# Graph layer with decayed neighbours: VectorE's differences taken straight behind the floors in every slot

## The chip, the cores and the metric

One core of one Trainium2 chip runs the kernel. The metric is the device time in microseconds (us) of one execution. An execution is measured from outside the profile; the span of the profile is the time from the first to the last recorded work of the core, and is a little shorter.

## The reference

The inputs are `x` (4096x64), a 0/1 matrix `adj` (4096x4096, about 16 ones in a row), a 64x64 weight and a bias, all float32. Cut to what matters:

```python
h = relu(layernorm(x))
support = h @ weight
mask = (adj != 0)
rank = cumsum(mask, axis=1)
deg = rank[:, -1:]
k = minimum(deg, 100)
pos = rank - (deg - k)
w = mask * where(pos > 0, 0.5 ** (k - pos), 0)
out = x + w @ support + bias
```

So each neighbour of a row is weighted by one half to the power of how many neighbours stand behind it. The running count, turned into powers of two, and the product with `support` are the work.

## The kernel before

**Tiling.** The rows of `adj` are taken in 32 groups of 128 (1 MB each). They are packed into 18 units (`SIZES`): units 0, 1, 2 and 17 hold one group, the others two. A unit's 4096 columns are walked backwards in steps of 128 columns, split into 2 or 4 chains side by side (`CHAINS`), so that a unit takes 16 (or 8) steps (`STEPS`).

**What the engines do for a unit.** GpSimd issues the load of a group (L242), eight in flight, each new one when `mask` has freed a buffer. VectorE makes 0/1 bytes of it (`mask`, L358), folds them with additions of halves (`halve_1`, `halve_2`, `halve_3`, all by L364), and scans the sums (`scan`, L399) to know how many neighbours stand behind each run of columns. TensorE starts a chain in PSUM from that (`base`, L612), and in each step adds the neighbours of one more block of columns (`count`, L624 and L626). ScalarE turns the PSUM values after each step into the bits of a power of two (`weigh`, L313, tile `powers`). TensorE multiplies these with `support` and adds up in a PSUM tile (`product`, L633, tile `acc`). `support` stands in three parts, whose three sums VectorE adds to `x` with `add_low`, `add_middle`, `add_high` (L436, L441, L446); then the rows are stored.

**Marked and plain groups.** `MARKS` says how many groups of a unit have their count marked by TensorE itself (two matmuls a step). The other groups, here called plain, are in units 5, 8, 11, 14, 15, 16 and 17. For them ScalarE writes powers of the running count alone, and VectorE makes weights of them in batches of four steps: `floor` (L415) raises values below a floor, in place, and `differ` (L425) subtracts each step's powers from the ones before. `differ` waits for `powers_ready` and for `floored`, which `floor` has signalled. A batch of four is one floor and one difference; there are 26 batches. TensorE's `product` waits for `weights_ready` ahead of each batch.

**The order of the work.** Every engine walks the same numbered slots `g`, in an order written out by hand. `STARTS[u]` is the slot in which TensorE does the base of unit u; the counts follow in the slots behind it, and the products of unit u begin `LAGS[u]` slots after its start. TensorE takes the chains of PSUM (`c = u % 3`) in order in each slot, and the first thing in a slot with products is what `before_products` waits for: for a unit's first product that is also `rows_done`, the `add_high` of unit u-4, whose `acc` tile it writes again. On VectorE batch j of unit u has its floor and its difference in slot `STARTS[u] + 4j + 5`; masks, halvings and scans of unit u stand 8 to 3 slots ahead of its start (shifted by `LEADS`), and the three additions in the slots `STARTS[u] + LAGS[u] + STEPS[u]`, one more and two more.

In this order the kernel before runs, in each slot on VectorE: the floors (L524 to L526), additions of the bias in two slots, then the masks, halvings, scans and additions of all units (L531 to L553), and last the differences:

```python
                for u in range(NU):
                    if MARKS[u] < SIZES[u] and g - STARTS[u] in range(BATCH[u] + 1, STEPS[u] + 2, BATCH[u]):
                        differ(u, (g - STARTS[u] - 1) // BATCH[u] - 1)
```

Of the kernel before, what the change touches and what calls it, by code (L numbers as in the profile page):

```python
# [5 lines left out]
def gnn_decay_kernel(nc, x, adj, weight, bias, out):  # L6
# [39 lines left out]
    SIZES = [1, 1, 1, 2, 2, 2, 2, 2, 2, 2, 2, 2, 2, 2, 2, 2, 2, 1]  # L46

    CHAINS = [4, 2, 2, 2, 2, 2, 2, 2, 2, 2, 2, 2, 2, 2, 2, 2, 2, 4]
    STEPS = [T // h for h in CHAINS]

    MARKS = [1, 1, 1, 2, 2, 0, 2, 2, 0, 2, 2, 0, 2, 2, 0, 0, 0, 0]

    STARTS = [0, 5, 6, 14, 23, 27, 34, 40, 45, 51, 57, 63, 68, 74, 80, 85, 91, 97]
    LAGS = [8, 5, 9, 10, 9, 10, 9, 8, 9, 8, 10, 12, 11, 11, 11, 10, 9, 8]

    BATCH = [4, 4, 4, 4, 4, 4, 4, 4, 4, 4, 4, 4, 4, 4, 4, 4, 4, 4]
# [4 lines left out]
    NU = len(SIZES)  # L61
# [7 lines left out]
    def taken_until(u):  # L69

        return sum(TAKEN[v] for v in range(u % FLIGHT, u, FLIGHT))

    def by_vector(u, b):
        return u in OWN_BEATS and OWN_BEATS[u][0] <= b < OWN_BEATS[u][1]
# [5 lines left out]
    def to_floor(u):  # L80

        if MARKS[u] == SIZES[u]:
            return []
        return [j for j in range(STEPS[u] // BATCH[u])
                if not all(by_vector(u, b) for b in range(first_of(u, j), BATCH[u] * (j + 1) + 1))]

    def floors_until(u):
        return sum(len(to_floor(v)) for v in range(u % FLIGHT, u, FLIGHT))
# [14 lines left out]
    with ctx:  # L103
# [110 lines left out]
        def plain(u):  # L214

            return slice(MARKS[u] * CHAINS[u] * P, SIZES[u] * CHAINS[u] * P)
# [133 lines left out]
        def _(dve):  # L350

            def mask(n):

                dve.wait_ge(adj_loaded[n % LOADS], 16 * (n // LOADS + 1))
                if n >= RING:
                    u = UNIT_OF[n - RING]
                    dve.wait_ge(chain_ready[u % FLIGHT], taken_until(u) + TAKEN[u])
                nc.vector.tensor_scalar(planes_of(n), in_planes(adj_b[:, n % LOADS, :], n), 0.0, 1.0,  # L358
                                        ALU.not_equal, ALU.mult).then_inc(mask_ready, 1)
# [11 lines left out]
            def halve_1(u):  # L371
                n, k = FIRST[u], SIZES[u]
                at = (n + SHIFT) % RING
                dve.wait_ge(mask_ready, n + k)
                halve(u, masks[:, at:at + k, :].bitcast(u16), words(part1, u, STEPS[u] // 4), halved)

            def halve_2(u):

                if CHAINS[u] == 4:
                    return  # L380
                dve.wait_ge(halved, halved_until(u) + 1)
                halve(u, words(part1, u, 4), words(part2, u, 2), halved)

            def halve_3(u):
                dve.wait_ge(halved, halved_until(u + 1))
                if u == 0:
                    dve.wait_ge(rests_ready, 2)
                if u >= SUMS:
                    dve.wait_ge(later_ready, FIRST[u - SUMS + 1])
                halve(u, words(part2 if CHAINS[u] == 2 else part1, u, 2),  # L390
                      runs_of(sums, sums_4, u)[:, :, 0:CHAINS[u] * P], sums_ready)

            def scan(u, k):

                dve.wait_ge(sums_ready, u + 1)
                if k == 0 and u >= SUMS:
                    dve.wait_ge(chain_ready[(u - SUMS) % FLIGHT], taken_until(u - SUMS) + 1)
                two = runs_of(sums, sums_4, u)[:, k, :].bitcast(u8).rearrange("q (r e) -> q e r", e=2)
                nc.vector.tensor_tensor_scan(runs_of(later, later_4, u)[:, k, ::-1], two[:, 0, ::-1], two[:, 1, ::-1],  # L399
                                             (OWN + STEP) / STEP if k < MARKS[u] else 0.0,  # L400
                                             ALU.add, ALU.add).then_inc(later_ready, 1)

            def weigh(u, b):

                c = u % FLIGHT
                dve.wait_ge(chain_ready[c], taken_until(u) + b + 1)
                nc.vector.tensor_scalar(powers[:, c, b, plain(u)].bitcast(i16), chain[c][:, plain(u)],
                                        (MAX_NEIGH + 1) * STEP, STEP, ALU.add, ALU.max).then_inc(powers_ready[c], 1)

            def floor(u, j):  # L410
                c = u % FLIGHT
                last = BATCH[u] * (j + 1)
                dve.wait_ge(powers_ready[c], taken_until(u) + last + 1)
                bits = powers[:, c, first_of(u, j):last + 1, plain(u)].bitcast(i16)
                nc.vector.tensor_scalar(bits, bits, STEP, None, ALU.max).then_inc(floored[c], 1)  # L415

            def differ(u, j):
                c = u % FLIGHT
                dve.wait_ge(powers_ready[c], taken_until(u) + BATCH[u] * (j + 1) + 1)
                done = floors_until(u) + sum(i <= j for i in to_floor(u))  # L420
                if done:
                    dve.wait_ge(floored[c], done)
                before = powers[:, c, BATCH[u] * j:BATCH[u] * (j + 1), plain(u)]
                after = powers[:, c, BATCH[u] * j + 1:BATCH[u] * (j + 1) + 1, plain(u)]
                nc.vector.tensor_tensor(before, before, after, ALU.subtract).then_inc(weights_ready[c], 1)  # L425
# [7 lines left out]
            def add_low(u):  # L433
                dve.wait_ge(acc_ready[u % ACCS], u // ACCS + 1)
                dve.wait_ge(xb_ready, 1 + (FIRST[u] + SIZES[u] > T // 4))
                nc.vector.tensor_tensor(sum_a[:, u % ACCS, 0:SIZES[u], :], parts_of(u)[:, :, 2, :], rows_of(u),  # L436
                                        ALU.add).then_inc(low_added[u % ACCS], 1)

            def add_middle(u):
                dve.wait_ge(low_added[u % ACCS], u // ACCS + 1)  # L440
                nc.vector.tensor_tensor(sum_b[:, u % ACCS, 0:SIZES[u], :], parts_of(u)[:, :, 1, :], sum_a[:, u % ACCS, 0:SIZES[u], :],  # L441
                                        ALU.add).then_inc(middle_added[u % ACCS], 1)
# [41 lines left out]
            def add_bias(f):  # L484

                dve.wait_ge(bias_ready, 1)
                rows = slice(0, T // 4) if f == 0 else slice(T // 4, T)
                n = rows.stop - rows.start
                nc.vector.tensor_tensor(x_sb[:, rows, :], x_sb[:, rows, :],
                                        bias_b.unsqueeze(1).to_broadcast([P, n, D]),  # L490
                                        ALU.add).then_inc(xb_ready, 1)
# [28 lines left out]
            for g in range(SLOTS + 4):  # L520
                for u in OWN_BEATS:
                    if by_vector(u, g - STARTS[u]):
                        weigh(u, g - STARTS[u])
                for u in range(NU):  # L524
                    if (g - STARTS[u] - 1) % BATCH[u] == 0 and (g - STARTS[u] - 1) // BATCH[u] - 1 in to_floor(u):
                        floor(u, (g - STARTS[u] - 1) // BATCH[u] - 1)  # L526
                if g == 15:
                    add_bias(0)
                if g == 46:
                    add_bias(1)  # L530
                for u in range(NU):  # L531
                    to = STARTS[u] - LEADS[u] - g
                    if u >= 3 and to == 8 and FIRST[u] > 3:
                        mask(FIRST[u])
                    if u >= 3 and to == 7 and SIZES[u] > 1:
                        mask(FIRST[u] + 1)
                    if u >= 3 and to == 6:
                        halve_1(u)
                    if u >= 3 and to == 5:
                        halve_2(u)  # L540
                    if u >= 3 and to == 4:
                        halve_3(u)
                    if u >= 3 and to == 3:
                        scan(u, 0)
                    if u >= 3 and to == 3 and SIZES[u] > 1:
                        scan(u, 1)
                    done = STARTS[u] + LAGS[u] + STEPS[u]
                    if g == done:
                        add_low(u)
                    if g == done + 1:  # L550
                        add_middle(u)
                    if g == done + 2:
                        add_high(u)  # L553
                for u in range(NU):
                    if MARKS[u] < SIZES[u] and g - STARTS[u] in range(BATCH[u] + 1, STEPS[u] + 2, BATCH[u]):
                        differ(u, (g - STARTS[u] - 1) // BATCH[u] - 1)

        @block.tensor
        def _(pe):
# [172 lines left out]
```

## Time and profile before

| what | value |
|---|---|
| median of 3 runs | 216.38 us (216.19 to 216.53) |
| the profiled execution, its own time | 216.8 us |
| span of the profile | 214.2 us |
| VectorE busy | 196.8 us, 239 instructions |
| TensorE matmuls busy | 196.7 us, 2784 instructions |
| ScalarE busy | 160.6 us, 303 instructions |
| loads of `adj` | 33.56 MB, 75.1% of the 16 DMA engines' span |

The granted clock of TensorE was full over the whole span. Busy time is the union of the recorded instructions; an engine that is busy all the time need not be the one that sets the end. What matters for a change of order is which engine waits for which, and how early each thing is ready before its user comes to it.

### The profile page before, as it was taken

The numbers are of one execution on the slowest core, as the hardware profiler recorded it, in microseconds if no ns is written. First come the engines' busy times: TensorE is split into PE (matmuls) and PEld (weight loads), VectorE is DVE, ScalarE is ACT, GpSimd is POOL, SyncE is SP. The second block draws the span as 40 slices with busy tenths as digits, with TensorE's granted clock in tenths as the row PEclk, the third lists the DMA queues.
The fourth block names the chain that finished last, engine by engine and source line by source line (L and its number), as shares of the span: only waits on it lengthen the run. The fifth ranks groups of instructions, "written<-read, shape, count | busy, mean of one in ns | idle before, by whom it ended". The sixth has DMA issues, their size and how long they took to land.

```text
span 214.2 us, 6505 instructions
## 1 busy us (share of the span) xinstructions
PE 196.7 (92%) x2784; PEld 188.0 (88%) x2784; DVE 196.8 (92%) x239; ACT 160.6 (75%) x303; POOL 29.1 (14%) x53
## 2 busy tenths in 40 slices
PE   0369979999999999999999999999999999999993
PEld 0269657997898999999999999999999999999993
DVE  1999979797979999999999999989999999998893
ACT  2442996786786988778778778789978989998720
POOL 7800000000010404010004110500000000000000
PEclk9999999999999999999999999999999999999999
DMA  6999999999999999999999999999998000000001
GB/s 203 204 217 220 216 211 216 216 219 212 218 213 221 210 218 216 213 220 216 211 222 212 217 218 215 216 217 218 221 209 174 8 12 3 12 15 3 17 0 43
DMA packets 7677, 36.09 MB, mean 168 GB/s; under 512 B 1506, under 2 KB 3298, under 8 KB 3554
## 3 DMA queue, kind: packets, MB, share of 16 engines
q0 software_dynamic: 4608, 33.56, 75.1%
q1 hardware_dynamic: 2882, 2.10, 3.8%
q8 instruction: 22, 0.36, 0.6%
q10 hardware_dynamic: 160, 0.03, 0.1%
q14 instruction: 5, 0.04, 0.1%
HBM read 68.19 MB, written 1.05 MB: 323 GB/s over the span
## 4 chain that ended last, share of the span: by engine, by line
PE 81%; DVE 7%; ACT 6%; DMA 2%; issue 1%; SPq 0%; DVEq 0%
PE acc L633 40%; PE chain L626 25%; PE chain L624 14%; ACT powers L313 3%; ACT support L296 3%; DMA x_sb<-in_x 2%; DVE masks L358 2%; PE chain L612 2%; DVE sq_sum L460 1%; DVE powers L455 1%; DVE later L399 1%; DVE row_sum L451 1%; DVE part L364 1%; DVE acc L481 0%; DVE sums L364 0%
## 5 line engine op out<-in xcount | busy, mean ns | idle before, releaser
L313 ACT ACTIVATE powers<-chain 128x512 int16<-128x512 f32 (+1 forms) x279 | 148.7, 573 | 33.6 <-PE chain L626 31.4
L633 PE MATMUL acc<-support,powers 128*128 128x192 bf16 x1024 | 159.5, 246 | 1.3 <-ACT powers L313 1.2
L626 PE MATMUL chain<-diag_own,masks 128*128 128x128 bf16 x608 | 107.1, 219 | 0.1
L624 PE MATMUL chain<-diag_past,masks 128*128 128x128 bf16 x568 | 102.2, 219 | 2.1 <-ACT powers L313 1.5
L633 PEld LDWEIGHTS acc<-support,powers 128*128 128x128 bf16 x1024 | 95.9, 98 | 4.3 <-ACT powers L313 2.4
L358 DVE TENSOR_SCALAR masks<-adj_b 128x4096 uint8<-128x4096 bf16 x32 | 72.6, 2281 | 5.0 <-DMA adj_b<-in_adj 5.0
L624 PEld LDWEIGHTS chain<-diag_past,masks 128*128 128x128 fp8e3 x568 | 55.5, 99 | 5.3 <-ACT powers L313 3.9
L626 PE MATMUL chain<-diag_step,masks 128*128 128x128 bf16 x416 | 60.1, 219 | 0.0
L626 PEld LDWEIGHTS chain<-diag_own,masks 128*128 128x128 fp8e3 x608 | 59.7, 99 | 0.3 <-issue 0.3
L626 PEld LDWEIGHTS chain<-diag_step,masks 128*128 128x128 fp8e3 x416 | 39.5, 99 | 0.0
L242 POOL DMA_DIRECT2D adj_b<-in_adj x32 | 24.5, 767 | 108.9 <-DVE masks L358 107.7
L425 DVE TENSOR_TENSOR powers<-powers 128x2048 bf16<-128x2048 bf16 x26 | 31.6, 1218 | 0.5
L399 DVE TENSOR_TENSOR_SCAN later<-sums 128x257 bf16<-128x257 uint8 (+1 forms) x32 | 21.6, 712 | 0.3
L415 DVE TENSOR_SCALAR powers<-powers 128x2048 int16<-128x2048 int16 (+1 forms) x26 | 18.7, 719 | 2.1 <-ACT powers L313 2.0
L364 DVE TENSOR_TENSOR part<-masks 128x2048 uint16<-128x2048 uint16 (+1 forms) x18 | 19.8, 1099 | 0.2
L577 PE MATMUL spare<-ident_f,powers 128*128 128x128 f32 x8 | 2.2, 425 | 9.6 <-DVE powers L455 8.8
L364 DVE TENSOR_TENSOR part<-part 128x1024 uint16<-128x1024 uint16 (+1 forms) x16 | 10.4, 651 | 0.2
L577 PEld LDWEIGHTS spare<-ident_f,powers 128*128 128x128 f32 x8 | 1.4, 216 | 9.9 <-issue 9.9
L296 ACT ACTIVATE support<-acc 128x512 bf16<-128x512 f32 x12 | 6.9, 647 | 1.2 <-DVE acc L481 1.2
L364 DVE TENSOR_TENSOR sums<-part 128x512 uint16<-128x512 uint16 (+1 forms) x18 | 7.3, 406 | 0.2
L451 DVE TENSOR_REDUCE row_sum<-x_sb 128x16 f32<-128x1024 f32 x2 | 2.4, 1220 | 5.1 <-DMA x_sb<-in_x 5.1
L612 PE MATMUL chain<-diag_base,later 128*128 128x128 bf16 x68 | 6.8, 220 | 0.0
(52 smaller groups left out, 66.3 us busy)
## 6 DMA issues: line engine op xcount, KB each, us to landing
adj_b<-in_adj POOLq DMA_DIRECT2D x32, 1024.0 KB, 35.0
x_sb<-in_x SPq DMA_DIRECT2D x2, 512.0 KB, 4.5
out<-x_sb SPq DMA_DIRECT2D x14, 64.0 KB, 5.4
out<-x_sb SPq DMA_DIRECT2D x4, 32.0 KB, 9.5
w<-in_L_gnn_weight ACTq DMA_DIRECT2D x2, 16.0 KB, 9.1
bias<-in_L_gnn_bias SPq DMA_DIRECT2D x1, 0.2 KB
```

The costliest lines, as they stand in the source:

```text
L242: pool.dma_start(adj_b[:, n % LOADS, :], adj_t[n]).then_inc(adj_loaded[n % LOADS], 16)
L296: nc.scalar.activation(steps_of(support[:, :, s, :], i), split[i][:, :].rearrange("p (t d) -> p t d", d=D), ACT.Copy).then_inc(part_ready[ ...
L313: nc.scalar.activation(powers[:, c, b, cols].bitcast(i16), chain[c][:, cols], ACT.Relu, bias=(MAX_NEIGH + 1) * STEP).then_inc(powers_ready ...
L358: nc.vector.tensor_scalar(planes_of(n), in_planes(adj_b[:, n % LOADS, :], n), 0.0, 1.0, ALU.not_equal, ALU.mult).then_inc(mask_ready, 1)
L364: return nc.vector.tensor_tensor(outs, ins[:, :, 0:h], ins[:, :, h:2 * h], ALU.add).then_inc(done, 1)
L399: nc.vector.tensor_tensor_scan(runs_of(later, later_4, u)[:, k, ::-1], two[:, 0, ::-1], two[:, 1, ::-1], (OWN + STEP) / STEP if k < MARKS[ ...
L415: nc.vector.tensor_scalar(bits, bits, STEP, None, ALU.max).then_inc(floored[c], 1)
L425: nc.vector.tensor_tensor(before, before, after, ALU.subtract).then_inc(weights_ready[c], 1)
L612: last = nc.tensor.matmul(chain[c][:, at:at + P], behind[:, hs - 1 - h], diag_base[:, :], start=(k + h == 0), stop=False, skip_group_check ...
L624: nc.tensor.matmul(chain[c][:, at:at + P], column(n, t + 1), diag_past[:, :], start=False, stop=False, skip_group_check=True)
L626: return nc.tensor.matmul(chain[c][:, at:at + P], column(n, t), diag_own[:, :] if marked else diag_step[:, :], start=False, stop=True, ski ...
L633: return nc.tensor.matmul(acc[u % ACCS][:, k * 3 * D:(k + 1) * 3 * D], powers[:, u % FLIGHT, s + 1 if k < MARKS[u] else s, at:at + P], sup ...
```

## The change

The loop over the differences moves, within each slot, from behind the masks, halvings, scans and additions to the place in front of them, behind the floors and the additions of the bias. No instruction is added or removed, and nothing moves to another slot or another engine.

```diff
                 if g == 46:
                     add_bias(1)
                 for u in range(NU):
+                    if MARKS[u] < SIZES[u] and g - STARTS[u] in range(BATCH[u] + 1, STEPS[u] + 2, BATCH[u]):
+                        differ(u, (g - STARTS[u] - 1) // BATCH[u] - 1)
+                for u in range(NU):
                     to = STARTS[u] - LEADS[u] - g
                     if u >= 3 and to == 8 and FIRST[u] > 3:
                         mask(FIRST[u])
...
                     if g == done + 2:
                         add_high(u)
-                for u in range(NU):
-                    if MARKS[u] < SIZES[u] and g - STARTS[u] in range(BATCH[u] + 1, STEPS[u] + 2, BATCH[u]):
-                        differ(u, (g - STARTS[u] - 1) // BATCH[u] - 1)
```

## Rows read from the trace of the kernel before

**Rows 1.** The page: busy by engine, and slices (tenths) of two engines and clock.
```profile
PE 196.7 (92%) x2784; PEld 188.0 (88%) x2784; DVE 196.8 (92%) x239; ACT 160.6 (75%) x303; POOL 29.1 (14%) x53
...
PE   0369979999999999999999999999999999999993
...
DVE  1999979797979999999999999989999999998893
...
PEclk9999999999999999999999999999999999999999
```

**Rows 2.** Busy time of each engine in three stretches of the span, by windows.
```profile
66.00:139.40 73.40, 72.71 (x1095) 71.60 (x1093) 73.23 (x85) 58.99 (x105) 14.27 (x13) 1.00 1.03 216
139.40:174.00 34.60, 34.60 (x535) 34.52 (x533) 33.84 (x41) 30.47 (x56) 0.00 (x0) 1.00 0.78 163
174.00:200.00 26.00, 26.00 (x377) 25.83 (x375) 25.15 (x35) 24.73 (x45) 0.00 (x0) 1.00 0.02 7
```

**Rows 3.** Who waited for whom: us in total, times, longest.
```profile
DVE powers L415 <- ACT powers L313: 2.0, 4, 0.8
...
PEld chain L612 <- DVE later L399: 0.6, 3, 0.2
```

**Rows 4.** The group of the differences, in the page's list of groups.
```profile
L425 DVE TENSOR_TENSOR powers<-powers 128x2048 bf16<-128x2048 bf16 x26 | 31.6, 1218 | 0.5
```

**Rows 5.** VectorE's timeline (start, us), slots 93 and 98, floors and differences.
```profile
182.64 0.68 DVE L415 TENSOR_SCALAR powers<-powers 128x2048 int16<-128x2048 int16 x1
183.24 0.28 DVE L446 TENSOR_TENSOR x_sb<-acc,sum_b 128x128 f32<-128x128 f32 x1
183.44 1.21 DVE L425 TENSOR_TENSOR powers<-powers 128x2048 bf16<-128x2048 bf16 x1
184.58 0.68 DVE L415 TENSOR_SCALAR powers<-powers 128x2048 int16<-128x2048 int16 x1
...
191.97 0.69 DVE L415 TENSOR_SCALAR powers<-powers 128x2048 int16<-128x2048 int16 x1
192.76 1.23 DVE L425 TENSOR_TENSOR powers<-powers 128x2048 bf16<-128x2048 bf16 x1
```

**Rows 6.** VectorE's timeline: two halvings in a row, and one with a difference behind.
```profile
64.88 0.69 DVE L364 TENSOR_TENSOR part<-part 128x1024 uint16<-128x1024 uint16 x1
65.60 0.43 DVE L364 TENSOR_TENSOR sums<-part 128x512 uint16<-128x512 uint16 x1
...
161.91 0.68 DVE L364 TENSOR_TENSOR part<-part 128x1024 uint16<-128x1024 uint16 x1
162.51 1.22 DVE L425 TENSOR_TENSOR powers<-powers 128x2048 bf16<-128x2048 bf16 x1
```

**Rows 7.** VectorE's timeline: unit 9's scans (slot 49) and the idle time in slot 72.
```profile
99.65 1.27 DVE L399 TENSOR_TENSOR_SCAN later<-sums 128x257 bf16<-128x257 uint8 x2
...
143.60 0.69 DVE L415 TENSOR_SCALAR powers<-powers 128x2048 int16<-128x2048 int16 x1 [0.65 <-ACT powers L313]
```

**Rows 8.** TensorE's timeline: base of unit 9 (slot 51) and first product of slot 95.
```profile
100.98 0.39 PE L612 MATMUL chain<-diag_base,later 128*128 128x128 bf16 x4
...
184.50 0.25 PE L633 MATMUL acc<-support,powers 128*128 128x192 bf16 x1
```

**Rows 9.** VectorE's timeline from slot 102: idle time ahead of two floors.
```profile
197.28 0.83 DVE L415 TENSOR_SCALAR powers<-powers 128x2560 int16<-128x2560 int16 x1 [0.41 <-ACT powers L313]
...
203.47 0.69 DVE L415 TENSOR_SCALAR powers<-powers 128x2048 int16<-128x2048 int16 x1 [0.77 <-ACT powers L313]
...
206.70 1.22 DVE L425 TENSOR_TENSOR powers<-powers 128x2048 bf16<-128x2048 bf16 x1
```

**Rows 10.** TensorE's timeline: four products across the start of slot 112.
```profile
208.78 0.49 PE L633 MATMUL acc<-support,powers 128*128 128x192 bf16 x4
```

## The prediction

> **What bounds the kernel now.** I read the page first. TensorE and VectorE are both busy 92% of the span, ScalarE 75%, TensorE's granted clock is full in every slice [rows 1], so busy time does not decide between the two. The stretches do part of it: between 66 and 139.4 us VectorE is busy 73.23 of 73.40 us, TensorE 72.71, and so it goes on to 200 us [rows 2]. The waits say who leans on whom. In the whole span TensorE's weight loads waited 0.6 us for VectorE's scans, and no wait for the differences or for the additions (which free `acc`) stands in the list; VectorE's floors waited 2.0 us for ScalarE [rows 3]. So TensorE sets the time, and VectorE keeps up with only scattered idle pieces. An instruction more on VectorE would be paid not at once but when the lead it works with is used up. The question for each thing VectorE makes is therefore how long before its use it is ready.
>
> The slot of an instruction follows from its place in the program order, counted through on both engines. By that, three leads matter:
> - The two scans of unit 9 end at 99.65 + 1.27 = 100.92, and the base of unit 9, first in slot 51, starts at 100.98 [rows 7, 8]. The 0.06 us between them is the shortest such distance that any user shows, so I take it as the signal's own time: this lead is zero.
> - `add_high` of unit 11 (slot 93) ends at 183.24 + 0.28 = 183.52 [rows 5]. It frees the `acc` tile of unit 15, whose products begin slot 95 at 184.50 [rows 8]. Less 0.06 the lead is 0.92 us.
> - The differences have more. The tightest I found, the last of unit 16, ends at 206.70 + 1.22 = 207.92, and TensorE reaches it no earlier than 208.78 [rows 9, 10].
>
> **What the change removes.** Nothing: the 26 differences, 31.6 us in all [rows 4], stay. Each is ready earlier within its slot. Since TensorE never waited for one and the tightest had over 0.8 us to spare, this is worth 0.
>
> **What it adds: places where an instruction stands right behind the one it reads.** VectorE's next instruction starts a little before the record of the last one ends, if it does not wait for it. A floor of 0.68 us is followed after 0.60 us by an addition that has nothing to do with it (182.64 to 183.24), but after 0.79 us by the difference that reads its result (191.97 to 192.76) [rows 5]. So a difference put straight behind its floor costs 0.19 us more. Five of the 26 stood there already, in slots without other work (89, 98, 100, 104, 106). Slot 102 has two floors and then two differences; only an addition between the pairs moves, so its two gain nothing either way. That leaves 19 new pairs, 15 of them up to slot 93. Seven floors are longer (0.83 us [rows 9] for five steps); none of these stood ahead of its difference, and I take the same 0.19.
>
> The differences also stood between other dependent instructions, and now these meet. Two halvings in a row start 0.72 us apart, 64.88 to 65.60, while one with a difference behind it gives way after 0.60 us, 161.91 to 162.51 [rows 6]: 0.12 us a pair. Going through the slots up to 93 I find six: the additions of unit 2 (slots 32/33), halvings 2 and 3 of unit 7 (36/37), 1 and 2 of units 12 (62/63) and 13 (68/69), 2 and 3 of units 15 (80/81) and 16 (85/86).
>
> Up to slot 93 VectorE so falls behind by 15 x 0.19 + 6 x 0.12 = 2.85 + 0.72 = 3.57 us. The one idle piece on the way, 0.65 us ahead of the floor at 143.60 [rows 7], absorbs 0.65, because ScalarE's result is by then late by less than that (1.0 us, next paragraph, against a delay of 2.19 us there). The rest, 2.92 us, arrives in slot 93. In other slots between 66 and 197 us VectorE runs without a pause.
>
> **Where it is paid.** First at the base of unit 9. Up to slot 44 there are four new pairs and two meeting ones, 0.76 + 0.24 = 1.00 us, and the lead is zero: TensorE is 1.0 us late from slot 51 on. Bases of later units had longer leads and keep up with it. Then in slot 93. There the order was floor, `add_high` of unit 11, difference; now it is floor, difference, `add_high`. The difference holds its place for 1.14 us (183.44 to 184.58 [rows 5]), the spacing of one behind which nothing waits. So `add_high` ends 2.92 + 1.14 = 4.06 us later (the 0.19 of slot 93's own pair is one of the 15). TensorE, which takes the lead of 0.92 first, starts slot 95 later by 4.06 - 0.92 = 3.14 us. The 1.0 us from slot 51 is inside this, not on top: VectorE's lateness does not depend on TensorE's, and the larger one counts.
>
> **What is behind the waiting instruction.** The products of unit 15 are the first thing in slot 95; all counts and products of the slot stand behind them, and ScalarE behind those. TensorE works without pause there (26.00 of 26.00 us [rows 2]), so it can't win it back. Behind slot 95 VectorE has its own four new pairs (units 15, 16, 14 and 16: 0.76 us), but the floors at 197.28 and 203.47 waited 0.41 and 0.77 us for ScalarE [rows 9], and the later scans and additions have leads of some 0.8 us against TensorE's new times, so I add nothing. Masks come up to 3 us later and with them the loads that GpSimd issues; the eight in flight cover that. The stores follow `add_high`; the last is behind TensorE's last product, as before.
>
> Sum: 3.57 - 0.65 + 1.14 - 0.92 = +3.1 us. Against the profiled execution that is a span of 217.3 us and 219.9 us in all; its 216.8 us stood 0.4 above the median, so the forecast for the median is 216.38 + 3.1 = 219.5 us.
>
> Bounds. The 0.19 could be as low as 0.12, what the meeting halvings show: 15 x 0.07 = 1.05 us less, +2.1. It could be 0.25 behind the longer floors, of which five come by slot 93: +0.3. The 1.14 is sure if the order is. If one more lead behind slot 95 gives way by a whole difference, +1.1. Below, the 1.0 us of slot 51 remains if slot 93 costs nothing.
>
> **A rule against it.** The rows show a start 0.19 us later behind a dependency. The Trainium skill, page "VectorE: DVE Perf Modes", section "The DRAIN you can't avoid", says otherwise: every VectorE operation is followed by an emptying of the pipe, and a chain with a semaphore after each operation took as long as one without, so that the semaphore "costs nothing extra here". By it the sum would keep only the displacement in slot 93. This trace disagrees for these forms, by the two spacings above.
>
> **The rivals.**
> 1. Standing behind one's producer costs nothing over a whole run, because the time shows up elsewhere anyway. Then only slot 93 is left: 1.14 - 0.92 = +0.2 us, 216.6. Against: 0.79 against 0.60 us, and 0.72 against 0.60, are plain spacings [rows 5, 6]. By the section of the Trainium skill named above, "VectorE: DVE Perf Modes", it would go this way.
> 2. The bases decide, not slot 93: VectorE's lateness is absorbed before 183 us, for example by idle time that opens when its data come late too. Then +1.0 us, 217.4. For: one such piece exists. Against: with TensorE only 1 us late, its results reach VectorE early.
> 3. VectorE becomes the bound to the end: a second lead behind slot 95 breaks. +3.1 + 1.1 = 220.6. For: slots 93 to 102 hold most floors and differences. Against: the 0.41 and 0.77 us of idle time there.
> 4. Faster: TensorE's pauses between 66 and 139.4 us, 73.40 - 72.71 = 0.69 us [rows 2], have no releaser in the list; were they batches of weights arriving late without the profile telling, earlier differences remove them, and if the added spacings stay inside the leads the time is 215.7. It decides only if the leads hold, which unit 9's does not.
>
> **How the numbers follow.** Forecast 0.65; rival 1 0.07, rival 2 0.13, rival 3 0.11, rival 4 0.04. A measurement can tell about 0.2% (0.43 us) from no change. Faster is rival 4: 0.04. Same is rival 1 and a little: 0.08. Slower is the rest: 0.88. The range runs from rival 2 to rival 3: 217.3 to 220.6.
>
> **What would show it.** Floor to difference spaced 0.79 us in nearly all batches; the scans of unit 9 about 1.0 us later and the base behind them, with TensorE waiting for L399; then one wait of some 2 us of TensorE's first product in slot 95, released by VectorE's L446; no new wait of ScalarE that isn't TensorE's. VectorE's busy time hardly changed, its lateness before slot 93 near 2.9 us. I am wrong if slot 95 starts less than 2 us later than before, or if TensorE's waits for VectorE lie in other slots.

## The result and the profile after

The changed kernel takes 219.97 us (median of 4 runs, 219.87 to 220.28), the kernel before 216.45 us (4 runs, 216.19 to 216.53). The ratio is 1.0167, with a 95% interval of 1.0152 to 1.0182: slower by 3.5 us. The forecast was 219.5 us.

First the page of the changed kernel: span, busy by engine, slices of TensorE and of the clock, and the group of the differences.

```profile
span 217.3 us, 6505 instructions
...
PE 197.4 (91%) x2784; PEld 188.9 (87%) x2784; DVE 199.0 (92%) x239; ACT 161.0 (74%) x303; POOL 32.0 (15%) x53
...
PE   0379979998999999999999999999999999699993
...
PEclk9999999999999999999999999999999999999999
...
L425 DVE TENSOR_TENSOR powers<-powers 128x2048 bf16<-128x2048 bf16 x26 | 31.8, 1225 | 2.5
```

Against [rows 1] no engine runs more instructions. VectorE's busy time grows by 2.2 us, most of it (1.8 us) because the starts that overlapped the record of the instruction before no longer do so behind a floor or between two dependent instructions that now meet. The differences themselves take 31.8 us as against 31.6 [rows 4]; what grew is the last number, the idle time just before them, from 0.5 to 2.5 us in all. In TensorE's slices one digit stands out, a 6 in the slice from 184.7 to 190.1 us. The clock is full.

The stretches (start:end, length, busy time of PE, PEld, DVE, ACT, POOL, clock, DMA) place the loss.

```profile
66.00:139.40 73.40, 72.58 (x1096) 71.64 (x1094) 72.29 (x83) 58.86 (x105) 16.46 (x13) 1.00 1.03 216
139.40:174.00 34.60, 34.24 (x522) 33.59 (x520) 34.01 (x39) 30.00 (x55) 0.72 (x1) 1.00 0.77 161
174.00:200.00 26.00, 24.11 (x351) 23.88 (x349) 24.96 (x35) 23.11 (x43) 0.00 (x0) 1.00 0.03 9
```

Between 174 and 200 us TensorE is busy 24.11 us where it was busy 26.00 [rows 2]. The waits of the changed kernel name what took it:

```profile
PEld acc L633 <- DVE x_sb L446: 2.1, 1, 2.1
...
PE acc L633 <- DVE x_sb L446: 1.9, 1, 1.9
PEld chain L612 <- DVE later L399: 1.4, 3, 0.7
...
DVE powers L415 <- ACT powers L313: 1.0, 3, 0.6
...
PE chain L612 <- DVE later L399: 0.8, 2, 0.5
```

The waits for L446 were not in the list before; they are one event, at the first product of slot 95. The waits for the scans were 0.6 us [rows 3]; now they are three events, at the bases of units 8 (slot 45), 9 (slot 51) and 15 (slot 85). Here TensorE's weight load at the base of unit 8, then its first matmuls at the bases of units 9 and 15 and in slot 95.

```profile
90.15 0.23 PEld L612 LDWEIGHTS chain<-diag_base,later 128*128 128x128 bf16 x4 [0.26 <-DVE later L399]
...
101.92 0.34 PE L612 MATMUL chain<-diag_base,later 128*128 128x128 bf16 x3 [0.50 <-DVE later L399]
...
167.56 0.40 PE L612 MATMUL chain<-diag_base,later 128*128 128x128 bf16 x4 [0.27 <-DVE later L399]
...
187.56 0.26 PE L633 MATMUL acc<-support,powers 128*128 128x192 bf16 x1 [1.89 <-DVE x_sb L446]
```

The base of unit 9 stood at 100.98 and slot 95 at 184.50 [rows 8]; the base of unit 15 stood at 166.56, 1.18 us behind the end of its scan, and now stands 0.06 us behind it (scans at 166.22, ending at 167.50). And VectorE around slot 93, to be laid beside [rows 5]:

```profile
185.29 0.69 DVE L415 TENSOR_SCALAR powers<-powers 128x2048 int16<-128x2048 int16 x1
186.08 1.23 DVE L425 TENSOR_TENSOR powers<-powers 128x2048 bf16<-128x2048 bf16 x1
187.22 0.28 DVE L446 TENSOR_TENSOR x_sb<-acc,sum_b 128x128 f32<-128x128 f32 x1
187.42 0.68 DVE L415 TENSOR_SCALAR powers<-powers 128x2048 int16<-128x2048 int16 x1
188.21 1.23 DVE L425 TENSOR_TENSOR powers<-powers 128x2048 bf16<-128x2048 bf16 x1
```

The floor starts 2.65 us later than before, the difference 0.79 us behind it, the addition 1.14 us behind that, and it ends at 187.50; TensorE's product starts 0.06 us later. From there on TensorE stands 3.1 us later than in the profile of before, to the end.

### The profile page after: what moved, and what is told of

It reads as the page before. It is cut to its first block, busy times and chain, and to the rows that moved or that the text cites. A ratio compares the mean times of both kernels' runs of the same rounds, so it can differ in the third digit from the quotient of the medians.

```text
span 217.3 us, 6505 instructions
## 1 busy us (share of the span) xinstructions
PE 197.4 (91%) x2784; PEld 188.9 (87%) x2784; DVE 199.0 (92%) x239; ACT 161.0 (74%) x303; POOL 32.0 (15%) x53
## 3 DMA queue, kind: packets, MB, share of 16 engines
HBM read 68.19 MB, written 1.05 MB: 319 GB/s over the span
## 4 chain that ended last, share of the span: by engine, by line
DVE 40%; PE 36%; issue 11%; ACT 5%; DMA 5%; POOL 1%; DVEq 0%; ACTq 0%; POOLq 0%
DVE masks L358 18%; PE acc L633 17%; PE chain L626 9%; PE chain L624 6%; DVE part L364 5%; DMA w<-in_L_gnn_weight 5%; DVE later L399 4%; DVE powers L415 4%; ACT powers L313 4%; PE acc L585 3%; DVE powers L425 3%; ACT support L296 2%; DVE sum_a L436 1%; DVE sum_b L441 1%; DVE x_sb L446 1%
## 5 line engine op out<-in xcount | busy, mean ns | idle before, releaser
L242 POOL DMA_DIRECT2D adj_b<-in_adj x32 | 27.4, 858 | 107.8 <-DVE masks L358 106.3
L425 DVE TENSOR_TENSOR powers<-powers 128x2048 bf16<-128x2048 bf16 x26 | 31.8, 1225 | 2.5
L585 PE MATMUL acc<-w,powers 128*128 128x128 f32 x32 | 6.5, 377 | 0.7 <-DMA w<-in_L_gnn_weight 0.7
```

The source lines that it names most:

```text
L242: pool.dma_start(adj_b[:, n % LOADS, :], adj_t[n]).then_inc(adj_loaded[n % LOADS], 16)
L585: last = nc.tensor.matmul(split[i][:, q * P:(q + 1) * P], h_t[:, 4 * i + q, :], w2[:, :], start=(q == 0), stop=True, skip_group_check=True)
```

## The experiments

Eight kernels, in two groups of four, each group on one chip with the kernel before (216.4 us in the first, 216.29 us in the second; the ratios are against these). Differences in us are worked out from the ratios.

**Slot 93 alone.** The kernel before, in which only slot 93 has the new order:

```diff
+                for u in range(NU):
+                    if (g == 93) and MARKS[u] < SIZES[u] and ...
+                        differ(u, (g - STARTS[u] - 1) // BATCH[u] - 1)
...
-                    if MARKS[u] < SIZES[u] and ...
+                    if not (g == 93) and MARKS[u] < SIZES[u] and ...
```

> The kernel before, with the difference taken ahead of the additions in slot 93 alone (unit 14's third batch against add_high of unit 11). Theory (leads): add_high of unit 11 starts 0.79 + 1.14 us behind its floor instead of 0.60, that is 1.33 us later, less the lead of 0.92: slot 95 and the end +0.4 us. Rival A (a difference right behind its floor costs nothing): 1.14 - 0.92 = +0.2 us. Rival B (VectorE is the bound, and each us added on it is paid, wherever it stands): only the added spacing, +0.2 us, with TensorE's slot 95 not late by one wait but by several small ones. The trace tells A from the theory by the spacing of floor and difference and by where slot 95 starts.

Measured: 216.66 us, ratio 1.0013 (1.0003 to 1.0022), +0.3 us. In its trace the floor starts at 182.03, the difference at 182.82 and `add_high` at 183.97: 1.94 us behind the floor instead of 0.60, as the theory had it, with one wait of 0.2 us of TensorE's weight load for L446. The time alone does not separate +0.4 from rival A's +0.2; the spacing of 0.79 does.

**All slots but 93.** The same edit with the condition turned round (`g != 93`).

> The changed kernel, with slot 93 alone in the old order. Theory (leads): VectorE comes to slot 93 some 2.65 us late as in the changed kernel; add_high of unit 11 is late by that less the lead of 0.92, so slot 95 is 1.7 us late; the scan of unit 17 then is 2.84 us late against a lead of 0.8, so slot 97 is 2.0 us late; the end +2.0 us against the kernel before, 1.0 under the changed kernel. Rival A (behind one's producer costs nothing): 0. Rival B (every added us on VectorE is paid): only 0.19 us below the changed kernel, +3.3.

Measured: 218.87 us, ratio 1.0116 (1.0101 to 1.0131), +2.5 us. Putting one addition back ahead of one difference returns 1 us, which rival B (0.2) can't give. In the trace slots 95 and 98 are 1.73 and 2.06 us later than in the profile of before, where 1.7 and 2.0 were expected (the base of unit 17 stands last in slot 97, so its wait shows from slot 98 on); the wait at slot 95 shrank from 1.9 to 0.5 us. Yet the measured total is 0.5 over the expected one. That gap came back in other kernels and is settled below.

**Unit 5's four batches alone** (condition `g <= 44`).

> The kernel before, with the differences ahead in slots up to 44 alone: the four batches of unit 5. Theory (leads): VectorE is 0.95 us late from slot 45 on, the base of unit 9 (slot 51) and TensorE with it 0.7 to 0.95 us late; TensorE's own pauses in slots 56 and 60, which the changed kernel no longer has, take most of that back, VectorE's lateness falls to 0.3 us at the idle piece of slot 72, and slot 93 has a lead of 0.92: the end 0.0 to +0.3 us. Rival B (every added us is paid): +0.95 us. Rival C (TensorE's lateness in slot 51 stays, since TensorE never pauses for anything it could win back): +0.7 to +0.95 us.

Measured: 217.09 us, ratio 1.0039 (1.0024 to 1.0054), +0.8 us. Here my theory missed and rival C's number fits. The time alone does not tell it from rival B's +0.95, which fell with the kernel above. In the trace, laid beside the second profile of the kernel before (below), TensorE is 0.44 us late ahead of slot 51, 0.88 us behind it and 0.76 us at the end: lateness that TensorE takes over there stays, but for 0.1 us. What had misled me was the first trace of before. Against it TensorE was 1.10 us late in slot 51 and only 0.29 us in slot 61, as if it had won the rest back in slots 56 and 60.

**One wait instead of two.** The changed kernel, with the redundant wait of `differ` taken out:

```diff
             def differ(u, j):
                 c = u % FLIGHT
-                dve.wait_ge(powers_ready[c], taken_until(u) + BATCH[u] * (j + 1) + 1)
                 done = floors_until(u) + sum(i <= j for i in to_floor(u))
```

> The changed kernel, in which differ waits for the floor's signal alone and no longer for powers_ready too (the floor has waited for the same value, so nothing is lost). Theory: of the 0.19 us behind a floor, 0.12 is the wait for the result, as between two halvings, and 0.07 the second wait instruction: spacing 0.72 us, 15 x 0.07 = 1.05 us less lateness in slot 93, the end +2.0 us against the kernel before. Rival: the second wait is handled while the floor runs and costs nothing; 0.19 is the price of this pair of forms: spacing stays 0.79 us and the end at +3.5 us as in the changed kernel.

Measured: 218.85 us, ratio 1.0114 (1.0096 to 1.0132): 1.1 us of the 3.5 are gone, as 15 x 0.07 = 1.05 us had it; the end itself is 0.5 us over the expected +2.0, the same gap as above. VectorE's timeline of this kernel in slot 93:

```profile
184.18 0.68 DVE L415 TENSOR_SCALAR powers<-powers 128x2048 int16<-128x2048 int16 x1
184.90 1.22 DVE L424 TENSOR_TENSOR powers<-powers 128x2048 bf16<-128x2048 bf16 x1
186.04 0.28 DVE L445 TENSOR_TENSOR x_sb<-acc,sum_b 128x128 f32<-128x128 f32 x1
```

0.72 us from floor to difference, as between two halvings [rows 6]. So the 0.19 us is 0.12 for the result and 0.07 for having two waits. The records of the trace show how (the timeline view leaves waits out): with two waits, the one for the floor's signal is recorded as an instruction of its own (0.02 us), and only the redundant one sits on the difference. In slot 93 of the changed kernel the wait stands at 186.01, 0.72 us behind the floor's start, where the difference itself stands with one wait, and the difference follows it by 0.07 us. In the old order this wait instruction ran while the addition was running (182.85, with the addition from 182.73 and the difference at 182.93, in the second profile below), and cost nothing. The one-wait kernel has 26 such wait instructions fewer, 75 instead of 101.

**The kernel before once more**, unchanged, for a second profile.

> The kernel before, unchanged, for a second profile of it. The forecast took the idle piece of 0.65 us ahead of the floor in slot 72 as a property of the kernel. In the profiles of the kernels so far, one that has the kernel's own order up to slot 93 among them, TensorE has no pauses in slots 56 and 60 (they were 0.46 and 0.28 us longer in the profile of before) and that idle piece is gone. Theory (the pauses are of that one execution): the second profile has slots 56 and 60 without them, VectorE reaches slot 72 without an idle piece of over 0.2 us, slot 93 comes some 0.6 us earlier on VectorE, and the span is 0.3 to 0.4 us shorter. Rival (they belong to this program, and the other orders remove them by delaying TensorE): the second profile shows them again, with the span at 214.2 us.

Measured: 216.36 us, ratio 1.0003 (0.9993 to 1.0013). Its span is 213.7 us. The stretches around slots 55 to 56 and slot 60, first in the profile of before, then in the second one:

```profile
108.60:113.60 5.00, 4.70 (x73) 4.50 (x69) 5.00 (x11) 3.81 (x8) 0.00 (x0) 1.00 1.04 217
119.00:122.00 3.00, 2.88 (x44) 2.68 (x42) 3.00 (x7) 2.29 (x5) 0.00 (x0) 1.00 1.03 214
```

```profile
108.60:113.60 5.00, 5.00 (x79) 5.00 (x77) 5.00 (x11) 4.28 (x8) 0.00 (x0) 1.00 1.03 216
119.00:122.00 3.00, 3.00 (x48) 2.96 (x46) 3.00 (x7) 2.50 (x5) 0.00 (x0) 1.00 1.06 220
```

The pause of slot 56 in the first profile, at TensorE's weight load, has no releaser:

```profile
111.67 0.10 PEld L624 LDWEIGHTS chain<-diag_past,masks 128*128 128x128 fp8e3 x1 [0.50 <-issue]
```

And VectorE at slots 72 and 93 of the second profile:

```profile
141.91 1.27 DVE L399 TENSOR_TENSOR_SCAN later<-sums 128x257 bf16<-128x257 uint8 x2
143.09 0.68 DVE L415 TENSOR_SCALAR powers<-powers 128x2048 int16<-128x2048 int16 x1
...
182.13 0.69 DVE L415 TENSOR_SCALAR powers<-powers 128x2048 int16<-128x2048 int16 x1
182.73 0.28 DVE L446 TENSOR_TENSOR x_sb<-acc,sum_b 128x128 f32<-128x128 f32 x1
```

The two pauses are all but absent (in the first profile the next slots came 0.46 and 0.3 us late by them), and the floor at 143.09 follows its scan without a gap: the idle piece of 0.65 us [rows 7] had been VectorE waiting, through ScalarE, for a TensorE that had just paused. Slot 93 comes 0.51 us earlier on VectorE, slot 95 and the end 0.46 us earlier on TensorE. This is what the theory of a property of one execution expected. No other trace of this study, that of the changed kernel among them, has a pause of that size in slots 56 or 60. Such pauses come and go elsewhere: of 0.2 us in slots 48, 56, 64, 73 and 77, and of 0.50 us in slot 77 of two other kernels, here of the one with slot 93 restored:

```profile
153.16 0.10 PEld L636 LDWEIGHTS acc<-support,powers 128*128 128x128 bf16 x1 [0.53 <-issue]
```

The second profile is free of the two that reached VectorE, and its span is that of the median run, so it is the right one to subtract from: unit 5 alone ends 0.29 + 0.46 = 0.75 us late (measured 0.8), all but slot 93 ends 2.06 + 0.46 = 2.5 (measured 2.5), one wait 1.90 + 0.46 = 2.4 (2.5), slot 93 alone -0.17 + 0.46 = 0.3 (0.3).

**Additions first.** In every slot behind the floors the additions, then the differences, then masks, halvings and scans:

```diff
+                for u in range(NU):
+                    done = STARTS[u] + LAGS[u] + STEPS[u]
+                    if g == done:
+                        add_low(u)
...
+                for u in range(NU):
+                    if MARKS[u] < SIZES[u] and ...
+                        differ(u, (g - STARTS[u] - 1) // BATCH[u] - 1)
                 for u in range(NU):
                     to = STARTS[u] - LEADS[u] - g
```

> In every slot the additions (low, middle, high) come right behind the floors, then the differences, then masks, halvings and scans. So every difference is still ahead of masks, halvings and scans, but eight of the fifteen pairs up to slot 93 have an addition between floor and difference, and add_high of unit 11 is ahead of the difference again. Theory (leads): VectorE is late in slot 93 by 7 x 0.19 + 5 x 0.12 = 1.9 us; less the lead of 0.9 and with no idle piece to absorb it, slot 95 is 0.7 to 1.0 us late, the end the same. Rival A (behind one's producer costs nothing): 0. Rival D (it is the masks, halvings and scans behind the differences that cost, each held back by 1.14 us): as the changed kernel, +3.5 us.

Measured: 217.39 us, ratio 1.0047 (1.0033 to 1.0061), +1.0 us. Every difference is still ahead of masks, halvings and scans, and 2.5 of the 3.5 us are gone, so their being held back is not the main cost. Against the second profile VectorE is 1.13 + 0.51 = 1.6 us late in slot 93 (1.9 expected), and TensorE 0.7 us late in slot 95 and 1.0 us from slot 98 on, by the scan of unit 17 (its base, the last in slot 97, starts 0.06 us behind it). TensorE's wait for L446 has shrunk to 0.1 us, too short for the list.

**Bias later.** The kernel before, with `if g == 46: add_bias(1)` turned into `g == 51`.

> The kernel before, with the addition of the bias to 24 rows (1.75 us on VectorE) moved from slot 46 to slot 51, behind the scan of unit 9, whose lead is zero. Theory (leads): the scan of unit 9 comes 1.66 us earlier, unit 10's scan at its old time, where the lead is 0.96; TensorE's wait of about 0.2 us at the base of unit 9 goes, the end -0.2 us (0.0 to -0.3). Rival B (VectorE's total is the bound): 0, since the same work stands on VectorE. Slower only if the first addition that needs the bias, unit 5's in slot 53, were late: it has the bias two slots ahead.

Measured: 216.12 us, ratio 0.9986 (0.9977 to 0.9995), about 0.2 to 0.3 us faster than the kernel before and the fastest of this study. Its scan of unit 9 is 1.66 us earlier than in the second profile of before, and TensorE's waits for scans fell from 0.8 us in the second profile to 0.3. The sign and size are as expected, though the gain is barely over what can be measured: in the trace TensorE gains 0.22 us in slot 51 against the second profile, and pauses of 0.2 us each in slots 56 and 77 take it back, so that only the median of 11 runs shows it.

**One wait in the kernel before** (the edit of the one-wait kernel, in the old order).

> The kernel before, with differ waiting for the floor's signal alone. Theory (leads): the five differences that stand right behind their floors there (slots 89, 98, 100, 104, 106) come 0.07 us closer, none of them on the path: 0.0 us. If the wait instruction cost time on VectorE wherever it stands, 26 x 0.07 = 1.8 us less on VectorE, and by rival B as much less in all.

Measured: 216.37 us, ratio 0.9999 (0.9986 to 1.0011): nothing. Since VectorE works with leads, the time alone would not show a saving there; the spacings do. The five differences right behind their floors came 0.07 us closer (0.72 instead of 0.79), the one in slot 32, behind an addition of 0.22 us, 0.05 us closer, and the other 20 not at all (0.60 us behind a halving, 1.14 us behind one of 1.22 us, 0.20 us behind an addition of 0.28 us, as with two waits). So the extra wait instruction costs only where it ends too late to be covered by the instruction ahead.

## Why the prediction was right

**What bounds the kernel.** TensorE sets the time and VectorE works with leads. Shown: where TensorE slips by VectorE (slots 45, 51, 85 and 95) is where a lead runs out, and its instruction then starts 0.06 us behind the end of VectorE's; unit 5's experiment shows that hardly any of a slip is won back.

**Differences ready earlier: 0.** No kernel gained from it; in both profiles of before the tightest difference was ready 1.10 us ahead of its product.

**19 pairs at 0.19 us, six meetings at 0.12 us.** The 0.19 us came out behind both kinds of floor: 0.79 us instead of 0.60 behind those of four steps, and behind those of five, which I could only bound, 0.93 us in slot 90 (179.89 to 180.82) instead of 0.73 with a mask behind it. The lateness that the 14 pairs and six meetings built up to the floor of slot 93 was forecast as 3.38 us. Measured against the second profile it is 2.65 + 0.51 = 3.16 us, and 0.27 more of it is hidden by VectorE having been that much earlier in slot 31, in the part of the run where it waits for loads: 3.43 us.

**The idle piece of slot 72, -0.65 us.** This term failed. It was the footprint of pauses of one execution: against the first profile VectorE's lateness did fall by 0.74 us there, and the sum's span of 217.3 us is the measured one, but against the second profile the term is 0. That is why the forecast of the median came out 0.4 us short: I moved the sum from the profiled execution to the median, 0.4 us lower, as if the difference between the two had nothing to do with any term, while it lay in this one.

**The base of unit 9, 1.0 us inside the total.** It stood 0.94 us later than in the profile of before, 0.7 us later than in the second one. That it is not added to slot 93's slip holds: against the second profile TensorE is 1.48 us late in slot 94 and 3.53 us in slot 95, whose product starts 0.06 us behind the end of `add_high`, so that VectorE alone sets it. The sentence that the bases of later units keep up is wrong. VectorE was 2.63 us late at the scan of unit 15, whose base had a lead of 1.12 us, and TensorE's lateness grew from 1.08 to 1.51 us in slot 85. The base of unit 8, ahead of unit 9's, had a lead of 0.29 us and slipped by 0.27 us in slot 45. I had listed neither, and TensorE waiting for VectorE in other slots is what I had named as a sign of being wrong. They cost nothing in the end because slot 95 takes more.

**Slot 93: +1.14 and -0.92.** `add_high` came 187.22 - 182.73 = 4.49 us later than in the second profile (4.06 forecast; the difference is that of the idle piece, less what VectorE was earlier in slot 31); the lead there was 184.03 - 183.01 - 0.06 = 0.96 us; slot 95 slipped by 3.53 us. That is the whole result, and the two experiments on slot 93 and the one-wait kernel take it apart: 1.0 us comes back with one addition ahead of one difference, 1.1 us with 0.07 us less a pair.

**Nothing behind slot 95.** Held: TensorE's slip is 3.06 to 3.08 us from slot 95 to the last, against the first profile. In the kernel with slot 93 restored the scan of unit 17 did take the next 0.33 us, so that lead was next in line as supposed.

**The rivals.** Rival 1 (standing behind one's producer is free) fell by the spacings and by the one-wait kernel. Rival 2 (lateness absorbed before slot 93) fell: VectorE was 3.16 us late there. Rival 3 (a further lead behind slot 95 breaks) is not seen; the one that broke unforeseen, unit 15's base, stands ahead of it. Rival 4 took TensorE's pauses for a cost of late weights; the largest are gone in the second profile of the same program, with the weights 0.2 us later in slot 54, not earlier, so they were not that. What makes TensorE pause in one execution and not in the next is open; the profile gives no releaser.

## What to carry to other kernels

On an engine that hardly idles but is not the bound, list for each product how long before its use it is ready, and price a reordering by the shortest leads, not by busy time: here a slack of 0.96 us was shortened by 4.49 us, which cost 3.5 us, though no work was added. List all of them: the bases of units 8 and 15 were not on my list and broke too. Keep an independent instruction between a producer and its reader on VectorE; "as early as possible" was the slowest of the orders tried for these differences, which had over 1 us to spare, and it pushed an addition that had less. Take a second profile of the same kernel before a gap of half a microsecond in the first one enters a sum, and make sure which gaps have a releaser: those of the bases do, the pauses don't.

## What the runs showed of the hardware

- VectorE's next instruction starts 0.60 us behind a floor of 0.68 us if it doesn't read it, 0.72 us if it waits for it with one wait, 0.79 us with two. This differs from the section of the Trainium skill cited in the prediction ("VectorE: DVE Perf Modes", "The DRAIN you can't avoid"), by which a chain with a semaphore after each operation took no longer than one with a semaphore only after the last: here 14 such pairs and six meetings of dependent instructions put VectorE 3.4 us back up to the floor of slot 93. Its chain was of other operations, and no run here repeats it.
- With two waits in front of a difference, one is an instruction of its own in the trace. Right behind the floor it waits for, the difference starts 0.07 us after it (slots 32 to 108 of the changed kernel, 0.065 or 0.066 us each time); behind 20 other instructions it is over in time and dropping it changes no spacing.
- From the end of a VectorE instruction's record to the TensorE instruction that waited for it 0.06 us pass, at the bases (units 8, 9 and 15 of the changed kernel) and at the product of slot 95 alike.
- TensorE can pause for 0.46 and 0.28 us without a releaser in one execution and not in another of the same program. VectorE idled for 0.65 us in slot 72 of that one. A pause of 0.50 us stood in slot 77 of two other kernels and not in either profile of the kernel before.
